# A fused graph and attention network on one core: attention's probability-times-value product as two products, one item later, and node rows in 500-byte tiles

## What is computed

```python
# feed-forward part of layer 0: softmax attention, 8 heads of 64, over all 625 nodes
scores = jnp.einsum('bhqd,bhkd->bhqk', q, k) / jnp.sqrt(jnp.float32(D_K))
attn = jax.nn.softmax(scores, axis=-1)
out = jnp.einsum('bhqk,bhkd->bhqd', attn, v)
...
# feed-forward part of layer 1: 128 anchors, one 512x512 matrix each
attn = jax.nn.softmax(scales / (distances + 0.1), axis=-1)
out = jnp.einsum('btn,btd,nde->bte', attn, x, value_weight)
```

## Time and profile before

| | |
|---|---|
| median of 3 runs | 2493.89 us (2493.52 to 2495.85) |
| profiled execution | 2496.94 us, span 2495.1 us |
| PE busy | 2382.2 us, 95% of the span |
| DVE, POOL, ACT busy | 70%, 64%, 37% |
| share of PE in the chain that ended last | 80% |

### The profile page before, as it was taken

How to read it: one execution, slowest core, us unless ns; L and a number is a source line. 1 busy time by engine, 2 the same in 40 slices (tenths; PEclk the granted TensorE clock), 3 DMA queues, 4 the chain that set the end, 5 groups by cost and what they waited for, 6 DMA issues and landing times.

```text
span 2495.1 us, 33879 instructions
## 1 busy us (share of the span) xinstructions
PE 2382.2 (95%) x11420; PEld 1972.0 (79%) x11420; DVE 1749.0 (70%) x2511; ACT 919.5 (37%) x1097; POOL 1602.4 (64%) x720
## 2 busy tenths in 40 slices
PE   6989979888999699999999999999999999999999
PEld 5878868776999577777777777777777777777777
DVE  8984235347998787777777777777777777777775
ACT  2841226622998622232323232232322322223221
POOL 0023413348887577777777777777777777777773
PEclk9998979999999999999999999999999999999999
DMA  3014110023444111212121212121212121212111
GB/s 77 20 55 158 46 68 18 1 77 76 122 103 110 40 68 68 101 67 101 67 101 67 101 67 101 67 101 67 101 67 101 67 100 68 97 71 94 74 68 38
DMA packets 49885, 190.85 MB, mean 76 GB/s; under 512 B 13300, under 2 KB 17911, under 8 KB 33444
## 3 DMA queue, kind: packets, MB, share of 16 engines
q1 hardware_dynamic: 35728, 177.90, 20.5%
q0 software_dynamic: 13200, 10.75, 2.1%
q10 hardware_dynamic: 900, 1.44, 0.2%
HBM read 177.54 MB, written 12.35 MB: 76 GB/s over the span
## 4 chain that ended last, share of the span: by engine, by line
PE 80%; DVE 13%; ACT 4%; issue 1%; POOL 1%; DMA 1%; SPq 0%; DVEq 0%; ACTq 0%; POOLq 0%
PE PS L1650 25%; PE PS L1651 24%; PE PS L1652 24%; PE PS L1861 2%; PE PS L1728 2%; DVE msgl L1456 2%; ACT msgh L1022 1%; DVE hotS L1149 1%; DVE hotD L1150 1%; DVE PS L1480 1%; DVE PS L1484 1%; DVE PS L1485 1%; DVE PS L1487 1%; DVE negmax L1363 1%; ACT PT L986 1%
## 5 line engine op out<-in xcount | busy, mean ns | idle before, releaser
L1594 DVE SCALAR_TENSOR_TENSOR XN<-PS,attn,XN 125x512 f32<-125x512 f32 x1083 | 804.6, 748 | 440.6 <-PE PS L1652 440.5
L789 POOL TENSOR_TENSOR OPl<-TS,OPh 128x1024 fp32r<-128x1024 f32 x256 | 679.0, 2653 | 123.6 <-ACT OPh L1041 116.8
L789 POOL TENSOR_TENSOR OPl<-RAW,OPh 128x1024 fp32r<-128x1024 f32 x192 | 556.8, 2900 | 256.6 <-ACT OPh L1041 256.6
L1650 PE MATMUL PS<-OPh,XVh 128*125 128x512 f32 x1280 | 508.0, 397 | 0.0
L1652 PE MATMUL PS<-OPh,XVl 128*125 128x512 f32 x1280 | 502.0, 392 | 0.0
L1651 PE MATMUL PS<-OPl,XVh 128*125 128x512 f32 x1280 | 501.1, 391 | 0.0
L1041 ACT ACTIVATE OPh<-TS 128x1024 fp32r<-128x1024 f32 x256 | 272.2, 1063 | 533.2 <-PE PS L1652 519.2
L1041 ACT ACTIVATE OPh<-RAW 128x1024 fp32r<-128x1024 f32 x192 | 203.6, 1061 | 583.3 <-PE PS L1652 577.2
L1650 PE MATMUL PS<-OPh,Sh 128*125 128x512 f32 x1024 | 404.0, 395 | 10.3 <-DVE XN L1591 10.1
L1652 PE MATMUL PS<-OPh,Sl 128*125 128x512 f32 x1024 | 404.7, 395 | 0.0
L1651 PE MATMUL PS<-OPl,Sh 128*125 128x512 f32 x1024 | 404.2, 395 | 0.0
(11 more groups left out here) (301 smaller groups left out, 3196.8 us busy)
## 6 DMA issues: line engine op xcount, KB each, us to landing
RAW<-in_values SPq DMA_DIRECT2D x64, 2048.0 KB, 7.7
filters<-filt SPq DMA_DIRECT2D x14, 672.0 KB
fil<-filters SPq DMA_DIRECT2D x11, 840.0 KB
Wraw<-in_ffn SPq DMA_DIRECT2D x4, 1024.0 KB, 6.0
Wraw<-in_L_q SPq DMA_DIRECT2D x2, 1024.0 KB, 5.0
Wraw<-in_L_k SPq DMA_DIRECT2D x2, 1024.0 KB, 8.3
Wraw<-in_L_v SPq DMA_DIRECT2D x2, 1024.0 KB, 7.2
gatW<-nodes,dstI POOLq DMA_INDIRECT x90, 3.4
```

The lines of the kernel that those rows point to most:

```text
L789: g.tensor_tensor(OPl[:, j], operand_source(j, parity), OPh[:, j].bitcast(F32), ALU.subtract).then_inc(op_lower, 1)
L1594: v.scalar_tensor_tensor(out=XN[:, t], in0=PS[0:P, bank, :], scalar=w, in1=XN[:, t], op0=ALU.mult, op1=ALU.add).then_inc(v_added, 1)
L1650: mm(dst, lh, rh, start=start, stop=False, skip_group_check=resumed)
```

## The change

- **Attention.** ACT puts the upper part of the probabilities into `PTh`, DVE the rest into `PTl` (`probT` is now in `SPLIT`, as is `v1`). `VS` replaces `VF`: per tile and pair of heads 256 columns, high and low values of the even head, then low and high of the odd one. `attn` is, for each of the five tiles, two fp32r matmuls with the same 128 stationary columns, by `PTh` and by `PTl`. Rows 64 to 127 of the result are the low values' share, so DVE needs two operations to take it (the rest, then the addition of the other half). `attn` is made one item later: at the steps where the turned item is number 4 of its head, and number 1 of the next.
- **Node rows.** `XVh`, `XVl` are gone and the anchors' plain rows are read from `XTh`, `XTl`; `Sh`, `Sl` hold 2 x 125 values side by side. All these tiles start 500 bytes apart. The buffers above them move down by 384 bytes; `below_OPh` keeps `OPh` at a multiple of 64 bytes.

```diff
-ATTENTION_STEPS = ITEMS + LAG + 1
+ATTENTION_STEPS = ITEMS + LAG + 2
...
-    if turned > 0 and turned % T == T - 2:
+    if turned > 0 and turned % T == T - 1:
         parts.append(("attn", turned // T * 2))
-    if turned > 0 and turned % T == 0:
+    if turned >= T and turned % T == 1:
         parts.append(("attn", turned // T * 2 - 1))
...
-BY_SCALAR = {"score", "v1", "probT", "qT2", "ov1"}
+BY_SCALAR = {"score", "qT2", "ov1"}
...
+        def value_parts(t):
+
+            pieces = VS[:, t].rearrange("p q (g d) -> p q g d", d=DH)
+            return pieces[:, :, 0:4:3], pieces[:, :, 1:3]
...
-                    a.activation(VF[:, tiles[0]:tiles[-1] + 1], slot(u)[0:P, 0:len(tiles), :], ACT.Copy).then_inc(drained_s, 1)
+                    for i, t in enumerate(tiles):
+                        ins = a.activation(value_parts(t)[0], by_parity(slot(u)[0:P, i]), ACT.Copy)
+                    ins.then_inc(upper_ready, 1)
...
-                    a.activation(PT[:, :, c], turned_tiles(u), ACT.Copy).then_inc(drained_s, 1)
+                    upper(u, PTh[:, :, c], turned_tiles(u))
...
                     if part == "attn":
                         head, h = n // 2, n % 2
                         o = 64 * (head % 2)
-                        rest(u, halves(XTl[o:o + 64, head // 2])[:, h], slot(u)[o:o + 64, 0, 0:HN], halves(XTh[o:o + 64, head // 2])[:, h])
+                        turned_l, low = halves(XTl[o:o + 64, head // 2])[:, h], 64 - o
+                        dve.wait_ge(upper_ready, splits(u))
+                        link(v.tensor_tensor(turned_l, slot(u)[o:o + 64, 0, 0:HN],
+                                             halves(XTh[o:o + 64, head // 2])[:, h].bitcast(F32), ALU.subtract))
+                        v.tensor_tensor(turned_l, slot(u)[low:low + 64, 0, 0:HN], turned_l.bitcast(F32), ALU.add).then_inc(drained_v, 1)
+                    if part == "v1":
+                        dve.wait_ge(upper_ready, splits(u))
+                        for i_, t in enumerate(TILES[n]):
+                            ins = v.tensor_tensor(value_parts(t)[1], by_parity(slot(u)[0:P, i_]), value_parts(t)[0].bitcast(F32), ALU.subtract)
+                        ins.then_inc(drained_v, 1)
+                    if part == "probT":
+                        c = tile_columns(n % T)
+                        rest(u, PTl[:, :, c], turned_tiles(u), PTh[:, :, c])
...
-                        ins = mm(slot(u)[:, 0, 0:HN], VF[:, t, c], PT[:, t, queries], start=t == 0, stop=t == T - 1)
+                        mm(slot(u)[:, 0, 0:HN], VS[:, t, head // 2, c], PTh[:, t, queries], start=t == 0, stop=False)
+                        ins = mm(slot(u)[:, 0, 0:HN], VS[:, t, head // 2, c], PTl[:, t, queries], start=False, stop=t == T - 1)
...
-                    return XVh[:, k, t, 0:P], XVl[:, k, t, 0:P]
+                    c = tile_columns(t)
+                    return XTh[:, k, c], XTl[:, k, c]
...
-                    return Sh[:, j, k, i, 0:P], Sl[:, j, k, i, 0:P]
+                    c = tile_columns(i)
+                    return Sh[:, j, k, c], Sl[:, j, k, c]
```

More of the change, by code:

```diff
@@ L51 @@
 ANCHORS = 128
-BELOW_SH = 8
 DUOS = ANCHORS // 2
@@ L111 @@
 UNITS += [(s, i) for s, n in (("length", 1), ("xt3", T), ("dist", 1), ("outT", T), ("final", 3)) for i in range(n)]
-BY_SCALAR = {"score", "v1", "probT", "qT2", "ov1"}
-SPLIT = {"xt0", "xwl", "kv0", "ct0", "xt1", "q1", "k1", "attn", "xt2", "kv2", "ct2", "xt3", "outT"}
+BY_SCALAR = {"score", "qT2", "ov1"}
+SPLIT = {"xt0", "xwl", "kv0", "ct0", "xt1", "q1", "k1", "v1", "probT", "attn", "xt2", "kv2", "ct2", "xt3", "outT"}
 WEIGHTS = [("L0_gnn_W_l", ("xwl", 2)), ("L0_q", ("q0", K - 1)), ("L0_gnn_W_r", ("xwr", 2)),
@@ L207, in build @@
         XN = sb("XN", [P, T, D], F32)
-        with ExitStack() as s:
-            XVh = sb("XVh", [128, K, T, 128], F32R, s)
-            XVl = sb("XVl", [128, K, T, 128], F32R, s)
         XTh = sb("XTh", [128, K, NT], F32R)
         XTl = sb("XTl", [128, K, NT], F32R)
-        sb("above_XT", [128, 2 * K * (T * 128 - NT)], F32)
         with ExitStack() as s:
@@ L312, in build @@
             keys_high = sb("keys_high", [128, HEADS, NT], F32R, s)
-            VF = sb("VF", [P, T, D], F32, s)
-            PT = sb("PT", [P, T, NT], F32, s)
-            sb("below_prob", [P, T * (D + NT) - 96], F32, s)
+            VS = sb("VS", [P, T, HEADS // 2, 256], F32R, s)
+            PTh = sb("PTh", [P, T, NT], F32R, s)
+            PTl = sb("PTl", [P, T, NT], F32R, s)
             prob = sb("prob", [P, 4, NT], F32, s)
@@ L352, in build @@
                 ov1T = sb("ov1T", [128, 3, NT], F32, s)
-            sb("below_Sh", [128, BELOW_SH], F32, late)
-            Sh = sb("Sh", [128, 4, 2, 2, 128], F32R, late)
-            Sl = sb("Sl", [128, 4, 2, 2, 128], F32R, late)
+            Sh = sb("Sh", [128, 4, 2, 2 * P], F32R, late)
+            Sl = sb("Sl", [128, 4, 2, 2 * P], F32R, late)
             XF = sb("XF", [128, K, T * P], F32, late)
@@ L369, in build @@
             attnsum = sb("attnsum", [P, T], F32, late)
-            sb("below_OPh", [128, 16], F32, late)
+            sb("below_OPh", [128, 24], F32, late)
             OPh = sb("OPh", [128, OPERANDS, 2, D], F32R, late)
@@ L487, in turned_tiles, with by_parity @@
             return slot(unit)[0:P].rearrange("p b (t n) -> p (b t) n", n=128)[:, 0:T, 0:P]
+        def value_parts(t):
+            pieces = VS[:, t].rearrange("p q (g d) -> p q g d", d=DH)
+            return pieces[:, :, 0:4:3], pieces[:, :, 1:3]
+        def by_parity(rows):
+            return rows.rearrange("p (q e d) -> p q e d", e=2, d=DH)
         def keys_low(head):
@@ L550, in count_fields @@
             return fields_a[:, s] if s < 2 else fields_b[:, s - 2]
-        def by_tile(columns):
-            return columns.rearrange("p k (i n) -> p k i n", n=P)
         def before(n, limit):
@@ L1063, in _ @@
                 a.activation(XF[:, :, tile_columns(j)], turned, ACT.Copy).then_inc(s_copied, 1)
-                upper(u, XVh[:, :, j, 0:P], turned)
+                upper(u, XTh[:, :, tile_columns(j)], turned)
             for j in range(T):
@@ L1070, in _ @@
                 act.wait_ge(s_summed, n + 1)
-                a.activation(Sh[:, j, :, :, 0:P], by_tile(SF[:, j]), ACT.Copy).then_inc(s_upper, 1)
+                a.activation(Sh[:, j], SF[:, j], ACT.Copy).then_inc(s_upper, 1)
             act.wait_ge(sq_ready, 1)
@@ L1132, in transposed_rest @@
                         v.tensor_copy(XTl[:, :, N:NT], XTl[:, :, N - 1:N].bitcast(F32).to_broadcast([128, K, NT - N])).then_inc(drained_v, 1)
-                    elif stage == "xt3":
-                        rest(u, XVl[:, :, j, 0:P], ins, XVh[:, :, j, 0:P])
                     else:
@@ L1357, in _ @@
                 ins.then_inc(drained_v, 1)
-            v.memset(PT[:, :, N:NT], 0.0).then_inc(pt_padded, 1)
+            v.memset(PTh[:, :, N:NT].bitcast(F32), 0.0)
+            v.memset(PTl[:, :, N:NT].bitcast(F32), 0.0).then_inc(pt_padded, 1)
             for i in range(ATTENTION_STEPS + 1):
@@ L1547, in _ @@
                 dve.wait_ge(s_upper, n + 1)
-                v.tensor_tensor(Sl[:, j, :, :, 0:P], by_tile(SF[:, j]), Sh[:, j, :, :, 0:P].bitcast(F32), ALU.subtract).then_inc(s_lower, 1)
+                v.tensor_tensor(Sl[:, j], SF[:, j], Sh[:, j].bitcast(F32), ALU.subtract).then_inc(s_lower, 1)
             dve.wait_ge(root_ready, 1)
@@ L1854, in _ @@
                     head, h = n // 2, n % 2
-                    u, c, queries = ("attn", n), slice(head // 2 * 128, head // 2 * 128 + 128), slice(h * HN, (h + 1) * HN)
+                    u, c, queries = ("attn", n), slice(head % 2 * 128, head % 2 * 128 + 128), slice(h * HN, (h + 1) * HN)
                     begin(u)
```

## The result

Side by side on one chip, the changed kernel takes 2520.14 us (median of 4 runs, 2519.58 to 2522.22) and the kernel before 2494.87 (4 runs, 2493.52 to 2499.34). The ratio is 1.0096, with a 95% interval of [1.0084, 1.0109]: 1% slower. The prediction was 2512, with a range of 2502 to 2532. The profiled execution is the one of 2522.22 us, 25.3 us above the one of before, where the sum had +18.5.

What follows compares the result with a forecast made beforehand. The prediction took a loop of waits to bound the attention and the matmul step the anchors. Its terms +15.8 + 5.9 - 3.2 + 0 = +18.5 us turned the median 2493.89 into 2512 us, range 2502 to 2532.

Steps and rivals of the forecast that it cites:

- What bounds it: Attention: no engine is full, a loop of waits sets the time, a head taking 13.32 us before the change.
- The product: Attention: ten fp32r matmuls take 1.58 us with the start, each product 1.14 us shorter, 16 of them 18.2 us.
- DVE's new work: Attention: each rest of a turned item out of PSUM takes DVE 0.80 us; taking `attn` 0.93 instead of 0.49.
- What becomes of the wait: Attention loop: PE waits for DVE's maximum, reciprocal and rest in four segments, 15.92 us a head against 13.28, +15.8 us.
- Start: Start of the attention: values' third part and first transposes wait for DVE, first product at 417.4 instead of 411.50, +5.9 us.
- End: End of the attention: 17.4 us instead of 20.6, since no scores are left in the loop, -3.2 us.
- Node rows: Anchors: 500-byte tiles cost no more than the mean of the two 512-byte ones, 0 us, ends -7.1 and +8.8.
- its rival: Attention heads: the clock falls to 1.2 GHz, 2524 us with a third of the heads, 2549 with all; chance 0.07.
- PE's saving comes through: Attention: the rests stay out of the loop and 16 products give -18.2, so 2476 us; chance 0.12.
- It cancels: Attention: only one of four segments per head meets its rest late, eating the saving, 2489 to 2498 us; chance 0.06.
- Slower tiles under load: Anchors: 500-byte tiles are slower with busy engines, every 3 ns more per step 21 us, 2533 us; chance 0.09.
- as summed: Whole kernel: the terms hold as added up, 2504 to 2520 us; chance 0.66.

Runs made afterwards that it cites:

- g: The changed kernel without the lower product, five matmuls for each product, DVE still making the rests; 2521.39 us, ratio 1.0107.
- e4: The changed kernel without the rests: `PTl` holds zeros, ACT's copy frees the slot, products keep ten matmuls; 2491.91 us, ratio 0.9975.
- v: The changed kernel with DVE making its rests from an SBUF copy; ACT's second copy frees the slot; 2510.17 us, ratio 1.0053.
- e1: The changed attention with node rows in 512-byte tiles as before, buffers 384 bytes lower; 2522.87 us, ratio 1.0113.
- f1: The kernel before with two fillers larger, so both distances from rows to operands are 64 modulo 512; 2489.3 us, ratio 0.9975.
- f3: The changed attention with 512-byte tiles and larger fillers, both distances from rows to operands at 64; 2507.86 us, ratio 1.0053.
- h runs: Three versions of the kernel before with other fillers, so other distances from rows to operands, one execution each; 2483.92, 2495.89 and 2508.45 us.
- h1: The kernel before with other fillers, distance 128 for the plain rows and 64 for the sums, one execution; 2483.92 us.
- e3: The changed kernel with the product at its old steps, not one item later; 2527.72 us, ratio 1.0123.
- w: The changed kernel with the rest outside the slot and node rows of 512 bytes at distance 64; 2494.42 us, ratio 0.9992.

## Why the prediction was right, and where it was off

- **What bounds it** (a loop of waits, not an engine): right. Nobody is full after the change either (PE 88 of 134 us, DVE 81), and the chain still alternates between engines.
- **The product**, 1.14 us shorter: right. From its first matmul to the maximum 451.50 - 449.19 = 2.31 us, where 2.36 was summed. g showed that it is in series.
- **DVE's new work**: 0.794 us for each rest, 0.80 taken, 0.72 of it on the path. The Trainium skill (VectorE: DVE Perf Modes, The TRN2 errata) has a row for operations out of PSUM from which the estimate is 0.776; the trace shows 0.794, and the measurement decides.
- **What becomes of the wait**: right in kind and size. Segments 3.95, 3.06, 3.97, 4.62 against 4.05, 3.13, 4.05, 4.69. A head is 15.60, and 15.81 every other time (433.38 to 449.19), 15.71 in the mean of six, where 15.92 was said: +14.6 in place of +15.8. e4 and v show the cause, the rest's place in the slot's loop. One detail was read wrong: that PE stands still some 1.7 us four times a head. Its waits in the timeline are 1.68, 1.13, 1.68 and 0.54 with 0.75 us, since PE has the next transposes to make inside the second and the fourth segment. The segments last as summed all the same, because the chain of waits runs through DVE's operations there.
- **Start**: +5.9 said, +7.4 measured from the values' first matmul to the first product (417.77 - 394.16, before 411.50 - 395.34). The third part came 2.5 us later, as said (402.76 - 394.16 against 401.47 - 395.34, 2.4 said). The other 1.6 us is the clock: it was at 0.52, the level of 1.2 GHz, over the 3.5 us of the second stretch above, right behind the stop of 2.28 us. The prediction named this as a sign of being wrong (PEclk leaving 1.00 between 395 and 530 us), and here it did, at the cost of these 1.6 us; the heads, where its rival had put the loss, stayed at 1.00.
- **End**: -3.2 said and measured, 529.50 - 512.04 = 17.46 against 20.69.
- **Attention together**: +18.8 against +18.5 (14.6 + 7.4 - 3.2). That it is so close is in part luck: the heads took 1.2 us less than said, the start 1.5 more.
- **Node rows**: this term was mis-sized, 0 said and **+5.5** measured, inside the ends of -7.1 and +8.8. The failed step is "500 bytes cost no more than the mean of the two 512-byte ones": it read the step of such tiles with other operands (`Wh`, `Wl`) and carried it over. The step is not a property of the tile: e1 has 512-byte tiles and the slower steps. By f1, f3 and the h runs it goes with where the two operands lie. Measured, 1396.7 / 6 = 0.2328 us, where 0.2322 was taken and the mean of before is 1392.6 / 6 = 0.2321; over the 1,152 groups of the anchors that is 4.7 of the 5.5. The reason given against a larger effect ("0.2312 to 0.2335 is all that the address moved so far") held: no layout left 0.230 to 0.234.
- **Rivals**: that PE's saving comes through would have needed the slot freed by another hand than DVE's; e4 shows what that gives (-11.9), at the price of the low probabilities. It cancels: fell, all four segments of a head met the rest. Slower tiles under load: the +21 us named did not come, and e1's 512-byte tiles under the same load took longer than the 500-byte ones.

The median lies 8 us above the forecast, at the upper edge of the prediction's own "as summed" (2504 to 2520): 5.5 from the anchors, 0.3 from the attention, 1.0 because the median of before is 2494.87 beside it and not 2493.89, and some 1 us from the other stages.

## What to carry to other kernels

When PSUM is emptied in two halves by two engines, the slot belongs to the slower queue: ask what stands ahead of the second half in that queue, and whether it needs the engine that waits for the slot. Work that is cheap by its amount (DVE is idle for 53 of the changed attention's 134 us) can stand in full on the path. And when a change moves buffers, take the layout's effect out first by putting the addresses back; here the layout alone moved the anchors by -11 to +9 us, and two larger fillers gave the only versions with all of the computation that are faster than both kernels (f1, and h1 in its one execution). Judge an experiment by its stage in the profile, not by its total: g's total had the wrong theory right.

## What the runs showed of the hardware

- **The step of fp32r matmuls of 512 columns depends on where their operands lie.** With PE never idle and the clock at 1.00, groups of six ahead of their own kind took 1380.0 ns (a step of 230.0) where stationary and moving operand lie 128 bytes apart modulo 512, 1386.2 to 1386.7 (231.1) at 64 and 320, and 1398.5 to 1400.0 (233.3) at the other five distances measured. The mean of one layout repeats within 0.1 ns from run to run (1386.7 in three kernels; 1397.2 and 1396.0 in the six with 500-byte tiles). Which unit makes it is open.
- **The granted clock fell in some heads of a loop and not in others.** In the changed kernel's loop it stays at 1.00 with PE busy 9.8 of 15.6 us. In g, with five matmuls fewer for each product, it was 1.00 in two heads and 0.62 to 0.89 in four. In v it was 0.81 over the end of the attention, and in w, whose attention is the same program, 1.00.
- **It fell behind a stop of 2.28 us.** At the attention's start, full matmuls behind this stop ran at 1.2 GHz for most of 3.5 us in the changed kernel (granted clock 0.52, 8 matmuls); behind the same stop it was 0.52 in e3 and 0.58 in f3 and g.
